# Up-projection from an exact ternary matrix in two passes plus a stacked rank part in one, in place of a summed weight split in two

## The reference, cut to what matters

```python
def _bitlinear(x, w_latent):
    scale = clip(mean(abs(w_latent), axis=1, keepdims=True), 1e-05, None)
    tern = clip(round(w_latent / scale), -1.0, 1.0)
    return x @ (tern * scale).T          # in value; w is tern
h = _bitlinear(x, w_fc) + gate * (x @ v.T @ fast_b.T @ u.T)   # w_fc [1024, 256], u [1024, 16], v [16, 256]
r = maximum(h, 0.0)
return _bitlinear(r * r, w_proj)         # w_proj [256, 1024]
```

## Time and profile before

| what | value |
| --- | --- |
| three runs | 954.75, 961.53, 962.61 us (median 961.53) |
| profiled execution | 957.39 us, its span 955.8 us |
| PE busy | 863.9 us, 90% of the span |
| PE weight loads busy | 718.4 us, 75% |
| DVE, ACT, POOL busy | 631.3, 479.1, 248.7 us |
| matmul records | 9972 |

### The profile page before, as it was taken

One profiled execution on the slowest core, in us unless ns is written; L12 is line 12 of the kernel. 1 busy time (PEld: TensorE's weight loads), 2 busy tenths in 40 slices (PEclk: granted clock), 3 DMA queues, 4 the chain that ended last, 5 costly groups with the idle time before them and its releaser, 6 DMA issues. The chain is left out here.

```text
span 955.8 us, 26466 instructions
## 1 busy us (share of the span) xinstructions
PE 863.9 (90%) x9972; PEld 718.4 (75%) x9973; DVE 631.3 (66%) x1025; ACT 479.1 (50%) x678; POOL 248.7 (26%) x268
## 2 busy tenths in 40 slices
PE   6846999999999973999999999999999999972995
PEld 3324888888888863888888888888888888862895
DVE  6882799898998973456555565565555655651885
ACT  5413677777777773333443343444434343334662
POOL 1022464664646601011121121111111111110111
PEclk9977899999999997999999999999999999985998
DMA  6272323324233129676778868778777687693897
GB/s 185 65 252 106 117 100 123 141 88 159 105 119 145 68 95 292 119 172 160 164 146 195 181 154 172 145 174 183 176 167 162 148 183 172 127 196 86 249 332 275
DMA packets 86705, 152.84 MB, mean 160 GB/s; under 512 B 12981, under 2 KB 62278, under 8 KB 85382
## 3 DMA queue, kind: packets, MB, share of 16 engines
q1 hardware_dynamic: 74902, 109.01, 47.2%
q0 software_dynamic: 11616, 42.21, 13.4%
q10 hardware_dynamic: 144, 1.05, 0.3%
HBM read 102.83 MB, written 49.41 MB: 159 GB/s over the span
## 5 line engine op out<-in xcount | busy, mean ns | idle before, releaser
L1080 PEld LDWEIGHTS py<-vwin,lead 64*64 64x64 f32 x5120 | 134.0, 134 | 35.8 <-issue 35.8
L965 DVE TENSOR_TENSOR r_lo<-r,r_hi 128x512 fp32r<-128x512 f32 x128 | 107.6, 840 | 78.8 <-ACT r_hi L1012 78.8
L1080 PE MATMUL py<-vwin,lead 64*64 64x128 f32 (+4 forms) x5120 | 147.8, 266 | 12.8 <-issue 12.7
L1012 ACT ACTIVATE r_hi<-r 128x512 fp32r<-128x512 f32 x128 | 80.8, 631 | 153.7 <-DVE r L960 153.7
L1009 ACT ACTIVATE r<-pf 128x512 f32<-128x512 f32 x128 | 76.5, 598 | 137.2 <-PE pf L412 132.7
L1061 PE MATMUL pp<-wproj,r_hi 128*128 128x256 f32 x512 | 135.9, 299 | 3.4 <-DVE r_lo L965 2.4
L1061 PE MATMUL pp<-wproj,r_lo 128*128 128x256 f32 x512 | 127.8, 282 | 0.0
L451 POOL TENSOR_SCALAR lead<-lead,norms 128x256 f32<-128x256 f32 x64 | 113.8, 1788 | 3.4 <-POOL norms L445 3.4
L1061 PEld LDWEIGHTS pp<-wproj,r_hi 128*128 128x128 f32 x512 | 96.9, 189 | 19.2 <-DVE r_lo L965 5.7
L611 DVE SCALAR_TENSOR_TENSOR xc<-ctrl,taps,xc 128x512 f32<-128x512 f32 x128 | 96.8, 776 | 18.8 <-ACT xc L683 18.1
L410 PE MATMUL pf<-tokens,split_a 128*128 (+1 forms) x256 | 101.3, 396 | 0.4 <-issue 0.4
(11 more groups left out here) (158 smaller groups left out, 1607.1 us busy)
## 6 DMA issues: line engine op xcount, KB each, us to landing
lead<-filters SPq DMA_DIRECT2D x128, 320.0 KB, 5.9
xnT_hbm<-split_b SPq DMA_DIRECT2D x32, 512.0 KB, 3.1
tokens<-xnT_hbm POOLq DMA_DIRECT2D x32, 512.0 KB, 7.0
lead<-in_attn_x SPq DMA_DIRECT2D x16, 512.0 KB, 3.8
gc_hbm<-xc SPq DMA_DIRECT2D x16, 512.0 KB, 2.6
xb<-in_attn_x POOLq DMA_DIRECT2D x16, 512.0 KB, 7.2
xf_hbm<-xb POOLq DMA_DIRECT2D x16, 512.0 KB, 3.8
GC<-gc_hbm SPq DMA_DIRECT2D x32, 256.0 KB, 7.4
```

The source lines that it names most:

```text
L965: dve.tensor_tensor(r_lo[j][:, :], r[j][:, :], r_hi[j][:, :].bitcast(F32), ALU.subtract).then_inc(r_split, 1)
L1012: act.activation(r_hi[j][:, :], r[j][:, :], ACT.Copy).then_inc(r_hi_done, 1)
L1080: last = pe.matmul(py[g % 2][q * BW:(q + 1) * BW, side, l, :, A:NB], tile[rows, q * PAIR + l, j * BW:(j + 1) * BW], vwin[g % 2][rows, q, l ...
```

## The change

The scale of a row of tern is a factor of a whole row of `h`, and the Relu commutes with it, so it moves behind the matmul: ACT's Relu gets `scale=fscale[:, m]`. What is left of the weight is -1, 0 and 1, exact in fp32r, so `fc` needs only tern·x_hi and tern·x_lo: four matmuls instead of six. The rank part is made apart. Once in an iteration `rank` multiplies the tokens with four stacked copies of the 16 rows of gate·fast_b·v (64 columns of weight, `vrank`, tile 128*64) in four matmuls of 512 columns into `zbank`, which lies in `py[1]`. ACT writes `zhi` from it (`rank_high`, with a mask that is 1 for one of the four copies), DVE subtracts (`rank_rows`) and leaves `zs`, 64 rows. In each unit a fifth matmul adds `ranks` (64 rows by 128 columns, u divided by the row scale, in parts) times `zs` to the four others. Its weight spans 64 rows of the array, so its tile is 64*128. In mix DVE's `low` of unit 7 moves behind the next iteration's `rank_rows`. The operands lie where the two halves of the summed weight lay.

In setup the eight matmuls of L354, the eight DVE sums and DVE's low part fall away; in their place come two small matmuls, four small DVE operations, eight transposes of `ustack` between the second and the third layer, and an ACT copy of `ranks` ahead of the third layer. HBM gets `fc_t` (1 MB), `u_t` (256 KB) and `v_t` (64 KB) in place of `fc_hi` and `fc_lo`.

```diff
@@ setup, sync
-            sp.wait_ge(weff_hi_ready, 1)
-            load(fc_hi, weff_hi[:, :, :].bitcast(F32), stored)
-            sp.wait_ge(weff_lo_ready, 1)
-            load(fc_lo, weff_lo[:, :, :].bitcast(F32), stored)
+            sp.wait_ge(ranks_ready, 1)
+            load(u_t, ranks.bitcast(F32), stored)
+            sp.wait_ge(ustack_ready, 2)
+            load(v_t, vrank[:, :, :, :].bitcast(F32), stored)
+            sp.wait_ge(ternT_ready, 1)
+            load(fc_t, tern.bitcast(F32), stored)
@@ setup, scalar
             act.activation(h2, lower, ACT.Gelu, bias=b2s[:, :]).then_inc(h2_ready, 1)
+            act.wait_ge(uT_mm, 1)
+            act.activation(ranks, upper[0:HALF, 0:HID], ACT.Copy).then_inc(ranks_ready, 1)
@@ setup, tensor
-            pe.wait_ge(rank_ready, 2)
-            for m in range(HT):
-                last = pe.matmul(ps[:, 4 + m // 2, (m % 2) * D:(m % 2 + 1) * D], uT[:, m * P:(m + 1) * P], m1[:, :],
-                                 start=True, stop=True)
-            last.then_inc(rank_mm, 1)
...
+            pe.wait_ge(ustack_ready, 2)
+            for m in range(HT):
+                last = pe.transpose(upper[0:HALF, m * P:(m + 1) * P], ustack[:, m, :, :].bitcast(F32).rearrange("p s r -> p (s r)"), ident[:, :])
+            last.then_inc(uT_mm, 1)
             pe.wait_ge(h2_ready, 1)
-            pe.wait_ge(tern_ready, 1)
+            pe.wait_ge(ranks_ready, 1)
@@ mix, vector
+            def rank_rows(it):
+                dve.wait_ge(z_hi_done, it + 1)
+                dve.tensor_tensor(zs, zbank, zhi.bitcast(F32), ALU.subtract).then_inc(z_ready, 1)
+
             def body(order, m, it, first):
+                rank_rows(it)
+                if not first:
+                    low(it - 1, HT - 1)
@@ mix, scalar
+            def rank_high(it):
+                act.wait_ge(z_mm, it + 1)
+                act.activation(zhi, zbank, ACT.Identity, scale=lowmask[:, :]).then_inc(z_hi_done, 1)
+
-            def activate(it, m):
+            def activate(it, m, last=False):
...
-                act.activation(r[j][:, :], pf[j][:, :], ACT.Relu).then_inc(relu_done, 1)
+                act.activation(r[j][:, :], pf[j][:, :], ACT.Relu, scale=fscale[:, m:m + 1]).then_inc(relu_done, 1)
+                if m == HT - 1 and not last:
+                    rank_high(it + 1)
@@ mix, tensor
                 for k in range(KT):
-                    tokens = [xm[:, bass.ds(even, 1), part, k, :].rearrange("p s t -> p (s t)") for part in range(2)]
-                    last = split_mm(pe, pf[m % 2][:, :], (wfc[0][:, k, ws], wfc[1][:, k, ws]), tokens, k == 0, k == KT - 1)
+                    for part in range(2):
+                        last = pe.matmul(pf[m % 2][:, :], tern[:, k, ws], tokens(even, part, k), start=(k == part == 0), stop=False)
...
-                last.then_inc(fc_mm, 1)
+                if m == 0:
+                    pe.wait_ge(z_ready, it + 1)
+                pe.matmul(pf[m % 2][:, :], ranks[:, ws], zs, start=False, stop=True).then_inc(fc_mm, 1)
+
+            def rank(it, even):
+                pe.wait_ge(vrank_in, 16)
+                pe.wait_ge(y_out, it * GPI + 2)
+                wait_alone(pe, xn_loaded, it * 32 + 32, pe_passed)
+
+                for k in range(KT):
+                    for part in range(2):
+                        last = pe.matmul(zbank, vrank[:, k, :, :].rearrange("p s r -> p (s r)"), tokens(even, part, k),
+                                         start=(k == part == 0), stop=(k == KT - 1 and part == 1))
+                last.then_inc(z_mm, 1)
...
+                        if g == 0:
+                            rank(it, m % 2)
```

More of the change, by code:

```diff
@@ L44, with setup_stage @@
 TIME_ROW = 64
-def setup_stage(nc, hbm, ident, bv_row, flag, V, GC1, Wv, Win, Wgate, eps, half, load_first, norm, weff):
+PARTS = 4
+HALF = PARTS * RANK
+def setup_stage(nc, hbm, ident, bv_row, flag, V, GC1, Wv, Win, Wgate, eps, half, load_first, norm, tern, ranks, fscale):
     (in_w, in_b, out_b, freqs, w1, b1, w2, b2, w3, b3, decay, gate_w, fast_b, w_fc, w_proj, u, v, gate,
-     filters, fc_hi, fc_lo, proj_t, scales) = hbm
+     filters, fc_t, u_t, v_t, proj_t, scales) = hbm
     with ExitStack() as ctx:
@@ L256, in ternary @@
                 return last
[L258 to L264, removed]
+            ternary(fc_nat, fc_tern, fsc, fth, HT, D).then_inc(tern_ready, 1)
+            dve.wait_ge(rank_in, 16 * RANK_LOADS)
+            link(dve.reciprocal(finv[:, :], fsc[:, :]))
+            link(dve.tensor_tensor(uscaled, us[:, :, :], finv[:, :].unsqueeze(2).broadcast_to([P, HT, RANK]), ALU.mult))
+            link(dve.tensor_copy(ustack, uscaled.unsqueeze(2).broadcast_to([P, HT, PARTS, RANK])))
+            dve.tensor_tensor(ustack[:, :, 1, :], uscaled, ustack[:, :, 0, :].bitcast(F32), ALU.subtract).then_inc(ustack_ready, 1)
+            dve.wait_ge(vrank_hi_done, 1)
+            dve.scalar_tensor_tensor(out=vrank[:, :, PARTS - 1, :], in0=ps[:, 4, 0:KT * RANK].rearrange("p (k r) -> p k r", k=KT), scalar=gcol[:, :],
+                                     in1=vrank[:, :, 0, :].bitcast(F32), op0=ALU.mult, op1=ALU.subtract).then_inc(ustack_ready, 1)
             def filter_tile(w):
@@ L347, in _ @@
             pe.wait_ge(ident_ready, 1)
-            for m in range(HT):
-                last = pe.transpose(ps[0:RANK, m // 4, (m % 4) * P:(m % 4 + 1) * P], us[:, m, :], ident[:, :])
-            last.then_inc(uT_mm, 1)
-            pe.matmul(ps[0:RANK, 2, 0:D], fbT[:, :], vs[:, :], start=True, stop=True).then_inc(m1_mm, 1)
-            pe.wait_ge(rank_ready, 2)
-            for m in range(HT):
-                last = pe.matmul(ps[:, 4 + m // 2, (m % 2) * D:(m % 2 + 1) * D], uT[:, m * P:(m + 1) * P], m1[:, :],
-                                 start=True, stop=True)
-            last.then_inc(rank_mm, 1)
+            for k in range(KT):
+                last = pe.matmul(ps[:, 4, k * RANK:(k + 1) * RANK], vs[:, k * P:(k + 1) * P], fbT[:, :], start=True, stop=True)
+            last.then_inc(m1_mm, 1)
             pe.wait_ge(filter_in, 16 * FILTER_LOADS)
@@ L379, in _ @@
             pe.wait_ge(h_ready, 3)
+            pe.wait_ge(tern_ready, 1)
             for k in range(KT):
@@ L1022, in body @@
                     activate(it, 2 * g)
-                    activate(it, 2 * g + 1)
+                    activate(it, 2 * g + 1, last and order == ORDERS - 1)
             window(0, 0, 0, 0)
+            rank_high(0)
             for order in range(ORDERS):
```

75 lines of the change are left out of this document (45 added, 30 removed).

## The result

The changed kernel takes **985.1 us** (median of four runs, 980.36 to 985.61), the kernel before beside it 962.07 (954.75 to 965.1): ratio 1.0231, 95% interval 1.0192 to 1.0269. Two later comparisons gave 1.0209 (1.0136 to 1.0281) and 1.0213 (1.0178 to 1.0248). So it is slower, as forecast, by 20 to 23 us where 14.5 were forecast, and 1.1 us above the range. The profiled execution took 984.90 us, 27.5 more than that of before, where the sum had 17.5. That sum gives 974.9 for an execution like the profiled one; the three runs before had their median 4.1 above it, so by the same sum a median is 979.0. I wrote 976 and gave no reason for the 3 us that I took off.

A forecast was written before the change was run, and what follows sets the result against it. PE was taken to bound mix, half of the span (busy 454.81 of 457 us). 957.39 + 20.7 (mix: -14.7 + 36.4 - 1.0) - 3.2 (setup) = 974.9 us; 976 was forecast as median, range 955 to 984.

The forecast's parts named there:

- the sum: Whole kernel: profiled execution 957.39 us, plus 20.7 for mix, minus 3.2 for setup, gives 974.9 us.
- The seams (part 2): PE in mix: changes of tile shape between neighbouring matmuls cost 0.19 us each (0.09 + 0.10); +36.4 us in all.
- Both faster rivals: Mix: change of rows is free, 944.7 us, chance 0.12; or drain paid but load hidden, 956.1 us, chance 0.13.
- The matmuls (part 1): PE in mix: fc loses 29.4 us of matmuls, rank adds 14.7, at 0.23 us each; net -14.7 us.
- The waits (part 3): Mix: PE's few waits for DVE shrink as groups get longer; -1.0 us, bounds -3 and 0.
- the z chain: Mix: from rank through ACT and DVE, zs is ready 2.5 us before the fifth matmul asks for it; no wait.
- the late z or another new wait: Mix: zs comes late, each further 0.1 us costing 1.6 us, 985 and more, or another new wait; chance 0.05.
- Setup (part 4): Setup: chain 1.5 us earlier and 1.7 us fewer stores; next stage's first transpose 3.2 us earlier, bounds 0 to 5.
- the bytes: End of setup: 704 KB fewer to store, worth 1.7 us.
- more if PE's clock stays up: Setup: the chain's gain of 1.5 us (0 to 2) could be larger if PE's clock stays up between layers; no size given.
- The rest: The stretches just ahead of mix and behind it: forecast change 0.

The follow-up runs named there:

- run 4: The kernel before with only the last of the six matmuls of each fc unit cut to 64 rows: 991.25 us, ratio 1.03.
- run 2: The changed kernel with the weight of fc's fifth matmul, and zs, filled with zeros to 128 rows: 953.97 us, ratio to the kernel before 0.9924.
- run 9: The changed kernel with 64 more PE instructions in a branch never taken and without POOL's bias addition: 976.36 us, one execution.
- runs 10 and 11: The kernel before: in 10, setup's eight rank matmuls moved behind the filters' first layer, 965.37 us; in 11, one rank matmul for eight, 956.01 us.
- run 1: The changed kernel again, no edit: 982.51 us.
- run 7: The kernel before with 64 more PE instructions in a branch never taken: 963.15 us.

## Why the prediction was wrong in size

**The seams (part 2): right.** Each change to or from 64 rows costs 0.09 us of drain and 0.10 of open load, some 180 times: +34.8 us in run 4 against 34.2, -30.0 to -33.5 in run 2. The 64-row matmul starts 0.32 us behind its forerunner and not 0.23. For this change the trace agrees with the Trainium skill, TensorEngine Tiling (Array Packing), Key Properties, by which a change of the tiling mode drains TensorE. The step from 128\*128 to 128\*64 is a change of mode by that page's list too, and there run 2 shows no drain (0.23 us). The weight loads stand idle 0.36 us each in 123 places ahead of the 64-row matmul. The Trainium skill's rule that a load into the background buffer may be pulled ahead, whatever its rows (TensorE: Matmul & The Clock Gate, Step-by-step), hides no load over this change. Both faster rivals are out. One detail of the reasoning was not right: I had taken the seams of the earlier trace rows for changes of rows and columns alike. Run 2 has 128\*128 to 128\*64 at 0.23 us, with no seam, so at least in that direction columns alone do nothing.

**The matmuls (part 1): right.** They take 0.23 us each. With 0.23 for the 64-row one too, its seams come to 0.09 and 0.10, and mix without the two disturbances below comes within 1 us of the sum.

**The waits (part 3): the step that failed.** I wrote that PE's few waits "shrink, since a group now is longer by some 0.3 us" and took -1.0, bounds -3 and 0. Mix exceeded the sum by 11.9 us in the first profile and by 8.4 to 10.3 in the two others. So the term "waits that this moves" was not -1.0 but about +7 to +11 us. It was two things. First and mostly, late instructions: I had no term for them, because the kernel before has only 0.6 and 0.3 us of such waits from 392 to 849 us, and gave the stage's length in instructions no thought. They are the long stalls at the two first passes (2.4 and 2.9 us, 1.5 for the clock behind the second), and with the code shifted mix is 6 to 9 us shorter. Second, POOL's addition: PE waits 3.1 us in 9 places for `r_lo` (392 to 870 us) where it waited 0.8 in 2 in the kernel before (392 to 849). `r_lo` isn't held more often, 8 times over 1.2 us against 12, and it isn't wanted sooner. In both profiles PE waits for a held `r_lo` only where it is that of unit 4, and only for what it takes over 2.2 us: in the changed kernel five of the eight are unit 4's and all five last longer (2.5 to 2.9 us, 2.5 of waiting in all; the four other waits are of 0.17 and stand behind no held one), in the kernel before four of the twelve are and two last longer (0.8 of waiting). In the second and third profile of the changed kernel these waits are 1.6 and 0.9 us. So what the held ones add over the kernel before is 0 to 2 us, and it hangs on when POOL's operation happens to start. Without the addition no `r_lo` takes over 1.2 us, and PE waits for one once at most (0.7 us in run 9). I named POOL as a danger for the z chain and not for the one that `proj` waits on, and gave "the late z or another new wait" a chance of 0.05. The z chain itself is as forecast, no wait in it.

**Setup (part 4): right sign, half the size.** -7.1 against -3.2, outside the bounds of 0 to 5. Parts by the trace, the kernel before and then the changed one:

```profile
26.43 6.75 PE L366 MATMUL ps_setup<-GC,w2s 128*128 128x512 f32 x8 [2.06 <-ACT GC L330]
...
35.23 15.98 PE L375 MATMUL ps_setup<-GC,w3s 128*128 128x512 f32 x32 [2.06 <-ACT GC L335]
...
54.15 1.97 PE L382 MATMUL ps_setup<-ident,V 128*128 128x128 f32 x16 [2.94 <-DVE V L271]
```

```profile
14.53 7.16 PE L362 MATMUL ps_setup<-GC,w1s 65*128 65x512 f32 x8 [6.84 <-ACT GC L325]
23.75 5.09 PE L366 MATMUL ps_setup<-GC,w2s 128*128 128x512 f32 x8 [2.06 <-ACT GC L334]
...
31.89 2.38 PE L379 MATMUL ps_setup<-GC,w3s 128*128 128x512 f32 x5 [2.11 <-ACT tokens L341]
...
49.08 2.40 PE L387 MATMUL ps_setup<-ident,V 128*128 128x128 f32 x16 [2.94 <-DVE V L279]
```

The first layer starts 2.6 us earlier (forecast 2.0 to 2.8) and `ranks` costs 1.0 (forecast 1.0). The second layer is 1.7 shorter, because the clock rose within it. The third is 1.7 shorter: over it the granted clock was 1.00 (31 to 47 us), where it had been 0.90 (35 to 52 us). That makes 5.1 at the transposes. The other 2.0 us lie behind the transposes (forecast 1.7 for the bytes); runs 10 and 11, which store all, keep 20.1 us there, but fewer bytes and DVE's missing low part are not told apart. So 3.4 of the 3.9 us of error are clock, which I had put in a parenthesis as "more if PE's clock stays up" and not into the bounds. Half of these 3.4, the second layer's, is luck of the profiled execution, as other executions show:

| profile | second layer | from third layer's start to the transposes | transposes |
| --- | --- | --- | --- |
| before | 6.75 | 18.9 | 54.15 |
| run 4 (setup as before) | 6.13 | 18.9 | 53.54 |
| changed, first | 5.09 | 17.2 | 49.08 |
| changed, second | 6.05 | 17.2 | 50.04 |
| changed, third | 6.69 | 17.2 | 50.69 |

The third layer's gain is in all three. It does not come from the rise within the second layer, which run 4 has too: in the kernel before the clock is down again at the start of the third layer (0.50 from 36.0 to 39.3 us, behind 2.1 us without a matmul) and its matmuls there are up to 0.85 us apart, in the changed one 0.43. They are 0.43 apart in runs 10 and 11 too, so this goes with the rank matmuls no longer standing ahead of the first layer; why is not shown. Run 11 gets only 0.5 of the 1.7, since its third layer has longer steps elsewhere.

**The rest.** The stage behind mix was 1.5 us longer in the profiles; over all profiles of either kernel with its edits it scatters from 99.9 to 106.4, so this is nothing to explain. On the profiled executions: -3.9 (setup), +11.9 (mix), +1.9 (rest) make the 10 us by which the sum was off. That the miss is not larger is luck: setup's unforeseen gain made up for a third of what mix lost. The range failed by 1.1 us on the median of that session; against the other two (982.5 and 981.9) it would have held. Its upper end was built from the seams, setup and scatter and had nothing for waits that grow, and it lay around 976 where my own sum made 979.0.

## What to carry to other kernels

A matmul of 64 rows among matmuls of 128 costs two changes of tile, 0.19 us each here. Filling the weight with zeros up to 128 rows left the steps at 0.23 us and took 28.5 us off this kernel. When a loop of PE was entered for the first time here, instruction transfers ran beside it, and whether they stalled PE depended on where the code lay: compare two kernels within half a per cent only with the instruction queue's transfers and the first passes in view, and try a shift in a branch that never runs. Profile an unaltered kernel more than once: the three profiles of this one differ by 3.5 us in mix and 1.6 in setup. Bound a term for "waits get fewer" on the side of more as well, whenever the order on DVE or the code's layout changes.

## What the hardware showed that I had not expected

- From tile 128\*128 to 128\*64 there is no seam (0.23 us), while 64\*128 after 128\*128 has 0.32, and what follows it 0.43, be it 128\*128 or 64\*64.
- Instructions come in 16 KB transfers on q8, in mix only in the first pass of its two loops (11 and 5 of them), and one that is late stops PE for 1.4 to 4.4 us. 64 more instructions that are never run changed mix by -5.8 us in the changed kernel (503.87 to 498.12) and by +3.2 in the one before (474.79 to 477.98, one execution each).
- Such a stall can also take the clock: behind 2.8 us of idleness PE ran its next eight `proj` matmuls (1.9 us for 1.05) and four of `fc` (1.7 us for 1.0) at about half pace, and the granted clock was 0.50. It fell behind 2.9 us (run 1) and 2.0 us (run 7) of idleness too, and stayed at 1.00 behind 2.6 us in the third profile.
- A POOL operation of 2.4 us on 128x1024 held a DVE operation from 0.7 to 2.7 us. In all 20 such places of the two profiles DVE's operation ends some 0.55 us after POOL's, so it gets done only when POOL's is over.
